# Issuing the second stage's one-time loads from ScalarE's queue instead of the sync queue, in a graph-network layer on one core

## What is computed

```python
def arma_conv(x, edge_src, edge_dst, init_w, w, root_w, b, num_layers=T):   # T = 3, K = 2 stacks
    deg = segment_sum(ones, edge_dst)
    dinv = where(deg > 0, deg ** (-0.5), 0.0)
    norm = dinv[edge_src] * dinv[edge_dst]
    root = einsum('nf,kfg->nkg', x, root_w)
    for t in range(num_layers):
        h = einsum(x, init_w) if t == 0 else einsum(out, w)
        msg = h[edge_src] * norm[:, None, None]
        h = segment_sum(msg, edge_dst, num_segments=n) + root + b[None]
        out = relu(h)
    return out.mean(axis=1)
...
h = relu(arma_conv(x, src, dst, init_w1, w1, root_w1, b1))        # 2 x 128 wide
latent = relu(arma_conv(h, src, dst, init_w2, w2, root_w2, b2))   # 2 x 64 wide
```

## Time and profile before

| | before |
|---|---|
| median of 3 runs, us | 3887.31 (3881.83 to 3890.51) |
| profiled execution, us | 3850.21 |
| its span, us | 3848.3 |
| TensorE busy, us and share of the span | 3540.3, 92% |
| TensorE idle before line 1316 in all, us | 27.6 |
| mean granted TensorE clock | 0.965 |

### The profile page before, as it was taken

One profiled execution on the slowest core, in us unless ns is written; L12 is line 12 of the kernel. 1 busy time (PEld: TensorE's weight loads), 2 busy tenths in 40 slices (PEclk: granted clock), 3 DMA queues, 4 the chain that ended last, 5 costly groups with the idle time before them and its releaser, 6 DMA issues. The chain is left out here.

```text
span 3848.3 us, 51302 instructions
## 1 busy us (share of the span) xinstructions
PE 3540.3 (92%) x18289; PEld 2013.8 (52%) x18290; DVE 1363.4 (35%) x4621; ACT 739.9 (19%) x1516; POOL 239.8 (6%) x255
## 2 busy tenths in 40 slices
PE   3898999999999699999989999999999998757999
PEld 2565455555545355555545555555555554535776
DVE  4445777767674111111111111211112002553444
ACT  0354444444442000000000000000000000432333
POOL 1000000000000000000000000000000000362333
PEclk9998999999999899999999999999999999878999
DMA  6121213131323799999964444898888995326775
GB/s 166 42 71 43 125 67 142 76 142 67 142 95 161 249 317 327 307 321 318 318 201 145 151 155 145 313 296 286 282 286 281 304 304 164 121 105 213 248 238 196
DMA packets 260290, 762.79 MB, mean 198 GB/s; under 512 B 25570, under 2 KB 176410, under 8 KB 258108
## 3 DMA queue, kind: packets, MB, share of 16 engines
q1 hardware_dynamic: 165360, 618.13, 47.0%
q10 hardware_dynamic: 83484, 115.15, 11.2%
q0 software_dynamic: 11312, 27.75, 2.0%
HBM read 533.28 MB, written 240.32 MB: 201 GB/s over the span
## 5 line engine op out<-in xcount | busy, mean ns | idle before, releaser
L1316 PE MATMUL acc<-ring,split 128*128 128x448 f16 x5488 | 1045.7, 353 | 27.6 <-DMA ring<-adj_d 27.6
L1316 PEld LDWEIGHTS acc<-ring,split 128*128 128x128 f16 x5488 | 537.6, 98 | 526.4 <-issue 31.5
L1316 PE MATMUL acc<-ring,other 128*128 128x448 f16 x4116 | 784.8, 353 | 0.0
L1034 PE MATMUL first_sum<-stage,other 128*128 128x448 f16 x2744 | 735.4, 357 | 2.5 <-DVE split L913 2.5
L1316 PEld LDWEIGHTS acc<-ring,other 128*128 128x128 f16 x4116 | 403.2, 98 | 378.4 <-issue 8.1
L1367 DVE TENSOR_TENSOR tmp<-acc,dinv_b 128x448 f32<-128x448 f32 x98 | 60.9, 622 | 1294.7 <-PE acc L1316 1294.7
L854 ACT ACTIVATE stage<-group_ps 128x392 f16<-128x392 f32 x784 | 383.1, 498 | 475.5 <-PE group_ps L1023 475.0
L900 DVE TENSOR_SCALAR place<-iota_col,rel 128x392 f16<-128x392 f16 x1568 | 427.5, 314 | 0.0
L1034 PEld LDWEIGHTS first_sum<-stage,other 128*128 128x128 f16 x2744 | 271.3, 99 | 225.9 <-issue 12.8
L1019 PE MATMUL group_ps<-place,lanes 128*128 128x392 f16 x784 | 268.2, 342 | 61.5 <-DVE place L900 48.6
L897 DVE TENSOR_TENSOR lanes<-iota_two,lane_two 128x256 f16<-128x256 f16 x784 | 224.6, 286 | 150.0 <-PE group_ps L1023 142.3
(11 more groups left out here) (331 smaller groups left out, 2596.6 us busy)
## 6 DMA issues: line engine op xcount, KB each, us to landing
ring<-adj_d SPq DMA_DIRECT2D x490, 784.0 KB, 4.3
adj_d<-stage SPq DMA_DIRECT2D x14, 5488.0 KB, 17.9
row_d<-blank ACTq DMA_DIRECT2D x20, 3340.5 KB, 58.0
slot_weights<-pack_d SPq DMA_DIRECT2D x42, 898.0 KB, 5.2
part_d<-blank ACTq DMA_DIRECT2D x10, 3340.5 KB, 59.6
slot_rows<-row_d SPq DMA_DIRECT2D x42, 393.0 KB, 5.9
rin<-root_d SPq DMA_DIRECT2D x28, 448.0 KB, 8.1
slot_base<-row_d SPq DMA_DIRECT2D x21, 393.0 KB, 5.8
```

What stands on the lines that cost most here:

```text
L1034: m = mm(acc[k][:, 0:WIN], other[:, h, half, k * P:(k + 1) * P], stage[:, b, h, :], start=(h == 0 and half == 0), stop=(h == TILES - 1 and ...
L1316: m = nc.tensor.matmul(acc[b][k][:, :], src[:, h, part, k * P:(k + 1) * P], ring[:, i, r, :], start=(h == 0 and part == 0), stop=(h == TIL ...
```

## The change

Eleven DMA issues and one wait move from the head of SP's list in the second stage to the head of ACT's. SP then begins with its loops over root rows and adjacency pieces. Transfers, sizes, semaphores and everything that waits for them are the same.

```diff
         with nc.Block() as block:
             @block.sync
             def _(sp):
-                sp.dma_start(split[:, (PAIRS - 3) * SUB:TILES, :, :], fresh_d[:, (PAIRS - 3) * SUB:TILES, :, :]).then_inc(c_last, 16)
-                sp.dma_start(dinv_b[:, :], dinv_d.rearrange("h (o p) -> o (h p)", o=1).broadcast_to([P, NP])).then_inc(b_in, 16)
-                sp.dma_start(w_one[:, :, :], a["L0_gnn_w1"].rearrange("k f g -> f k g")).then_inc(c_in, 16)
-                sp.wait_ge(c_z, 1)
-                for k in range(2):
-                    q = slice(H * k, H * k + H)
-                    sp.dma_start(w_two0[:, q], a["L0_gnn_init_w2"][k]).then_inc(c_in, 16)
-                    sp.dma_start(w_rtwo[:, q], a["L0_gnn_root_w2"][k]).then_inc(c_in, 16)
-                    sp.dma_start(w_two[q, q], a["L0_gnn_w2"][k]).then_inc(c_in, 16)
-                    sp.dma_start(b_two[q, :], a["L0_gnn_b2"][k].rearrange("(g o) -> g o", o=1)).then_inc(c_in, 16)
-
                 for t in range(LAST_PASS + 1):
...
             @block.scalar
             def _(act):
                 act.sem_inc(r_cp, 1)
+                act.dma_start(split[:, (PAIRS - 3) * SUB:TILES, :, :], fresh_d[:, (PAIRS - 3) * SUB:TILES, :, :]).then_inc(c_last, 16)
+                act.dma_start(dinv_b[:, :], dinv_d.rearrange("h (o p) -> o (h p)", o=1).broadcast_to([P, NP])).then_inc(b_in, 16)
+                act.dma_start(w_one[:, :, :], a["L0_gnn_w1"].rearrange("k f g -> f k g")).then_inc(c_in, 16)
+                act.wait_ge(c_z, 1)
+                for k in range(2):
+                    q = slice(H * k, H * k + H)
+                    act.dma_start(w_two0[:, q], a["L0_gnn_init_w2"][k]).then_inc(c_in, 16)
+                    act.dma_start(w_rtwo[:, q], a["L0_gnn_root_w2"][k]).then_inc(c_in, 16)
+                    act.dma_start(w_two[q, q], a["L0_gnn_w2"][k]).then_inc(c_in, 16)
+                    act.dma_start(b_two[q, :], a["L0_gnn_b2"][k].rearrange("(g o) -> g o", o=1)).then_inc(c_in, 16)
+
                 act.wait_ge(c_z, 2)
```

## The result

The change makes the kernel slower by about 15 us. The medians of eight runs each are 3882.68 us before and 3898.95 after, the ratio 1.0038 with a 95% interval of 1.0025 to 1.0051, that is 14.8 us (9.7 to 19.8); the two medians by themselves lie 16.3 apart. A second comparison, on another occasion, gave 1.0035 (1.0022 to 1.0048). The time of 3898.95 is inside the range of 3883 to 3902, the change is three times the forecast of 4.9 us, and it is on the rival of even shares (14.4 us).

What follows compares the result with a forecast made beforehand. TensorE bounds the second stage, idle only in one 27.6 us gap of transfer time before its first ring-piece matmul. Median 3887.3 plus 4.9 us for later weights gave 3892.2 us, range 3883 to 3902.

Steps and rivals of the forecast that it cites:

- the forecast of 4.9 us: Second-stage start: ScalarE's queue gets 2 to 4 packets to SyncE's one, TensorE starts 4.9 us later; chance 0.38.
- the rival of even shares: TensorE's wait for weights: engines give both queues equal packets or bytes, weights trail, 14.4 us lost, time 3901.7; chance 0.22.
- The worst order: Second-stage start: everything on SyncE's queue served first, 6.54 MB ahead of the weights, TensorE starting 14.4 us later.
- the fourth, "I take 2.48": Queue sharing at the stage start: 2.48 ScalarE packets to one of SyncE's, weights at 1290.7, start 4.9 us later.
- the 3.4: Packet ratio, ScalarE's queue to SyncE's, read beside the blank rows in the earlier trace: 5989 to 1746.
- "Pieces were queueing": Ring pieces beside ScalarE's small expert weights: claimed queued yet given fewer packets, landing in 8.5 us against 4.2 alone.
- the 5.9 to one: Packet ratio, ScalarE's queue to SyncE's, read beside the load of x: 1808 to 309.
- the mix: Second-stage start: one for one while packets are large, then 0.127 us per small one; start 9.1 us later; chance 0.12.
- The second way of the working: Weights' landing: 64 small packets at 0.127 us each, plus 0.9 us for rin packets; 6.7 us later, at 1290.6.
- "Nothing in the second stage can be gained ... except in that gap": Second stage: queue order can gain only in TensorE's 27.6 us idle gap before its first ring-piece matmul.
- The bounds of the change: TensorE's start in the second stage: from 1.3 to 2.0 us gained in the best order to 14.4 us lost.

Runs made afterwards that it cites:

- e3: Changed kernel with the nine small weights first on the sync queue, ScalarE issuing its two large loads only once they landed; ratio 0.9987 to the kernel before.

## Why the prediction was right and wrong

**Right: what bounds the stage, and the place of the loss.** TensorE started 13 us later (22.4 to 35.4), nothing was gained by queuing the pieces early (0.0 us idle before all other matmuls of line 1316, as before), and ScalarE's eleven issues cost nothing. The worst order was priced at 14.4 us; the lag grew by 12.9, the stage by 13.2 where the waits are out of the way, the whole time by 13.6 and 14.8 (the two ratios). TensorE began at the lower clock both times: 0.50, 1.2 GHz, from 1295 to 1300. From the start of the stage to the first relu it lost 13.3, 0.4 more than at the first matmul. TensorE worked at 0.50 from 1286.3 to 1291.5 before, and from 1295.1 to 1301.0 after, and then at 1.00 (2.4 GHz); 0.7 us more at the lower level are worth about that (an estimate).

**Wrong: the share of the queues.** The step that failed is the fourth, "I take 2.48". The true ratio is one to one (353 to 356, 50 to 50, 251 to 254), and the rival of even shares was the case. I had read ratios from the earlier trace rows as if the engines had chosen them. There SyncE's queue moved what TensorE consumed: in the earlier trace rows 8.70 MB in 58 us are 150 GB/s, and a piece of 803 KB for 28 matmuls, which e3 shows to take 5.47 us, is 147. In the earlier trace rows, where the 2.48 comes from, 11.88 MB in 42 us are 283 GB/s, and 283 is also what SyncE's queue moved alone in the stretch of the earlier trace rows. A queue that gets all it asks for says nothing of the share that it would get. The same trace of before has even turns inside those stretches, if it is read in single microseconds (1357 to 1358, 1359 to 1360, then 2446 to 2447, 2442 to 2443):

```profile
q10 hardware_dynamic: 124, 0.19, 107.5%
...
q1 hardware_dynamic: 45, 0.28, 79.2%
q10 hardware_dynamic: 47, 0.07, 23.8%
...
q10 hardware_dynamic: 473, 0.21, 73.1%
q1 hardware_dynamic: 35, 0.13, 30.7%
...
q1 hardware_dynamic: 61, 0.36, 86.0%
q10 hardware_dynamic: 60, 0.05, 15.2%
```

Over the whole of the earlier trace rows, in the half microseconds in which SyncE's queue moves at least 16 packets of a piece (27 us of 58), it is 1415 packets of SyncE's to 1628 of ScalarE's; in the rest it is 331 to 4361. While a piece is being moved it is nearly one for one, between two pieces ScalarE's queue has the engines nearly to itself, and the mean of both is the 3.4. In the earlier trace rows the same count is less clean, 1987 to 3753 over 34.5 us of 42: some of ScalarE's packets there have 24 bytes or fewer, and they pass by hundreds in a microsecond. That they pass on engines which hold none of SyncE's at that time fits, but is not shown, since the trace does not name a packet's engine. "Pieces were queueing" in the prediction does not hold at the engines: they were issued, but for most of the longer wait their packets had not begun. Counted off in order, 128 to a piece, a piece's ninth packet starts 1.1 us after its issue and its last 3.5 with SyncE's queue alone, 4.0 and 6.8 in the stretch of the earlier trace rows, 4.6 and 7.2 in that of the earlier trace rows (medians). Most of the later landing, 8.5 us instead of 4.2, thus lies ahead of a piece's packets and not between them. What holds them there stays open, and so does the 5.9 to one of the earlier trace rows.

**Wrong: the count of packets.** ScalarE's queue holds 8 + 8 large packets per engine, not 16 + 16, and each transfer adds one per engine: 91 for ScalarE's (1456 in the trace, 16 x 91), 97 for SyncE's, instead of 96 and 88. The 256 packets over 8 KB that it cites from the earlier trace rows are 16 per engine in all, not 32. In the sum of even shares the two mistakes cancel: by turns 91 of the 97 pass, nearly all of the 6.54 MB. In the mix they do not: 16 of SyncE's beside the large ones, all root rows, cost 1.2 us and not 5.2. The second way of the working, whose agreement with the first was chance, 0.127 us for a small packet, is off too: 73 packets took the weights from 1279.2, where the scales landed, to 1294.7, about 0.21 us each, because each took its turn with a piece's 6.3 KB.

**Missed: the wait of line 1291.** "Nothing in the second stage can be gained ... except in that gap" was read from the groups of line 1316 alone. The 12.9 us at line 1291 stood in the same trace. It did not bend the result (it does not depend on the lag), but removing it was worth more than anything done with the queues at the boundary: 11.9 us.

**The size of the confidence.** The bounds of the change, 2.0 us sooner to 14.4 later, were right and held what the lag and the stage lost. That the time lies inside 3883 to 3902 is in part luck: the range was built on 3887.3, the later runs put the kernel before at 3882.68, and on 3887.3 a change of 14.8 us would have come to 3902.1. Most of the chance, 0.63, went to a change within 7.8 us, and that was not the case. The chance for even shares, 0.22, was too low for the only case that had both the byte shares of the earlier trace rows and a stated rule behind it, against ratios from stretches in which one queue was not pressed.

## What to carry to other kernels

When two queues had packets at the engines, here, the engines took one of each in turn. So a set of many small packets that someone waits for should not run beside a queue of large ones: each of them pays for one large packet. Put what is awaited first, alone if it is small, and cut large transfers that run beside urgent ones into packets no larger than theirs. A ratio between queues may only be taken as a share where both are pressed; first compare each queue's rate with what its consumer eats, and look at stretches as short as one transfer, since a mean over 40 us mixes the time with both queues and the time with one. And before saying that a stage has one gap, list the idle time of every line of the bounding engine, not that of its main line.

## What the runs showed of the hardware

- Where two queues both had packets at the engines, these passed one for one, whichever of the two held the large ones, and whether the sizes were 21 KB to 1.8 (106 to 106), 6.3 KB to 0.3 (356 to 353), or 3 KB to 6.3 (251 to 254). The 5.9 to one of the earlier trace rows is not explained.
- Beside ScalarE's traffic a ring piece began to move 4.0 to 4.6 us after its issue, and 1.1 us after it with SyncE's queue alone.
- Each transfer adds one packet on each of the 16 engines: 1168 for nine transfers of 1024 rows.
- One part of the program (routing, with its 98 indirect transfers) takes 247 to 250 us in some executions and 291 to 297 in others, by chip and not by kernel as far as these runs show: 45 us in 3880, three times the effect that was to be measured.
